# A fused recurrent-attention kernel: another order for the start of its first stage, hinted loop branches, moved transfers and key products

## What is computed

```python
xn = _layernorm(x, axis=-1)
s = _L0_attn_ref(xn, ...)          # recurrent attention, then a gated MLP
g = _silu(_L0_ffn_ref(xn, ...))    # 8 low-rank experts, softmax gate
x = x + s * g
# in _L0_ffn_ref
h = jax.nn.relu(jnp.einsum('bsd,de->bse', x, W1) + b1)
alpha = jax.nn.softmax(jnp.einsum('bse,ek->bsk', h, W2) + b2, axis=-1)
vx = jnp.einsum('krd,bsd->bskr', V, x)
uvx = jnp.einsum('kdr,bskr->bskd', U, vx)
out = jnp.einsum('bsk,bskd->bsd', alpha, uvx)
# in _L0_attn_ref: q, k, gk (decay), v, g from rmsnorm(x); then per token
S = S * jnp.exp(gt)[..., None] + kt[..., None] * vt[..., None, :]
ot = jnp.einsum('bhk,bhkd->bhd', qt, S)
```

## Time and profile before

| what | value |
|---|---|
| runs | 1780.17, 1783.14, 1783.19 us; median 1783.14 |
| profiled execution | 1781.37 us, its span 1779.6 us |
| TensorE busy | 1652.1 us, 93% of the span |
| VectorE, ScalarE, GpSimd busy | 48%, 32%, 10% |
| mean granted clock of TensorE | 0.980 |

### The profile page before, as it was taken

The page is one execution under the profiler, slowest core; times in us unless marked ns, Lnnn a source line. Parts: engine busy times, 40 slices in busy tenths (PEclk is TensorE's granted clock), DMA queues, the critical chain, the costliest instruction groups (busy, mean ns, idle before and its releaser), DMA issues. The chain is left out here.

```text
span 1779.6 us, 30533 instructions
## 1 busy us (share of the span) xinstructions
PE 1652.1 (93%) x12304; PEld 1291.5 (73%) x12304; DVE 847.2 (48%) x1348; ACT 562.3 (32%) x959; POOL 172.4 (10%) x201
## 2 busy tenths in 40 slices
PE   4999999869999999999996499999999999999998
PEld 3777777647767767677675387878787878787886
DVE  3655455336776857758564455232242414141413
ACT  3333333225544625435242343122212121212110
POOL 5780000021010010110000000000000000000000
PEclk9999999989999999999997799999999999999999
DMA  7243333020022020120110322303030303020110
GB/s 152 81 124 95 82 85 93 24 83 32 2 79 79 1 79 27 53 79 1 74 37 13 124 89 101 118 0 118 0 118 0 118 0 118 0 92 26 34 61 24
DMA packets 49100, 111.87 MB, mean 63 GB/s; under 512 B 12704, under 2 KB 24048, under 8 KB 40816
## 3 DMA queue, kind: packets, MB, share of 16 engines
q1 hardware_dynamic: 45104, 89.44, 15.7%
q10 hardware_dynamic: 2304, 16.78, 2.3%
q0 software_dynamic: 1600, 4.25, 1.2%
HBM read 76.89 MB, written 33.57 MB: 62 GB/s over the span
## 5 line engine op out<-in xcount | busy, mean ns | idle before, releaser
L1255 DVE TENSOR_TENSOR m_h<-m_ps,m_silu 128x512 f32<-128x512 f32 x88 | 60.8, 691 | 426.5 <-PE m_ps L1405 426.5
L1403 PE MATMUL m_ps<-m_xshi,m_w1hi 128*128 128x512 f32 x352 | 143.4, 407 | 7.3 <-DVE m_xslo L1248 6.0
L1331 ACT ACTIVATE m_silu<-m_ps 128x512 f32<-128x512 f32 x88 | 52.5, 597 | 289.6 <-PE m_ps L1405 288.8
L1403 PE MATMUL m_ps<-m_xshi,m_w3hi 128*128 128x512 f32 x352 | 140.4, 399 | 2.3 <-ACT m_silu L1331 2.3
L1404 PE MATMUL m_ps<-m_xslo,m_w1hi 128*128 128x512 f32 x352 | 139.8, 397 | 0.0
L1405 PE MATMUL m_ps<-m_xshi,m_w1lo 128*128 128x512 f32 x352 | 139.6, 396 | 0.0
L1404 PE MATMUL m_ps<-m_xslo,m_w3hi 128*128 128x512 f32 x352 | 139.5, 396 | 0.0
L1405 PE MATMUL m_ps<-m_xshi,m_w3lo 128*128 128x512 f32 x352 | 139.5, 396 | 0.0
L855 POOL TENSOR_TENSOR row<-row,a_r 128x512 f32<-128x512 f32 x32 | 41.6, 1335 | 618.0 <-DMA a_r<-scratch_r 618.0
L1376 POOL TENSOR_TENSOR m_sq_sum<-m_sq 128x512 f32<-128x512 f32 x8 | 10.4, 1298 | 782.8 <-ACT m_sq L1314 782.8
L1403 PEld LDWEIGHTS m_ps<-m_xshi,m_w1hi 128*128 128x128 f32 x352 | 66.5, 189 | 26.6 <-issue 9.2
(11 more groups left out here) (247 smaller groups left out, 3844.9 us busy)
## 6 DMA issues: line engine op xcount, KB each, us to landing
row<-scratch_xn SPq DMA_DIRECT2D x16, 1024.0 KB, 5.2
row<-scratch_xmid SPq DMA_DIRECT2D x16, 1024.0 KB, 7.2
m_xt<-in_L_attn_W SPq DMA_DIRECT2D x33, 256.0 KB, 3.2
f_xt<-in_L_attn_x SPq DMA_DIRECT2D x8, 1024.0 KB, 10.2
scratch_xn<-row SPq DMA_DIRECT2D x8, 1024.0 KB, 8.9
scratch_gate<-row ACTq DMA_DIRECT2D x8, 1024.0 KB, 3.9
scratch_xmid<-row ACTq DMA_DIRECT2D x8, 1024.0 KB, 3.9
row<-scratch_gate SPq DMA_DIRECT2D x8, 1024.0 KB, 9.7
```

Source lines behind the costliest of these rows:

```text
L1255: dve.tensor_tensor(h[n], dense.region(f"b{j}"), silu[n], ALU.mult).then_inc(dense.taken_sem(f"b{j}"), 1)
L1331: act.activation(silu[n], dense.region(f"a{j}"), ACT.Silu).then_inc(dense.taken_sem(f"a{j}"), 1)
L1403: pe.matmul(ps, wh, xh, start=k == 0, stop=False)
```

## The change

1. The constants move into the first stage's own GpSimd program. ScalarE and TensorE wait only for the first three steps (identity, epsilon); the block and its meeting are gone.
2. Each row of x is loaded by four transfers of 128 tokens, and VectorE's statistics wait for each piece alone. V is loaded second, before b1; b2 last. ScalarE waits for b1 alone.
3. V is turned after the first hidden product and U after the third; ScalarE splits them before the second and the fourth result. TensorE's passes over non-existent results move ahead of the turning of x or behind U.
4. All loops of all engines are opened with a hint for the branch at their end (line 139 before).
5. In attention `k1` moves to chunk 0, `q0` to chunk 1, and `q1` stays alone in chunk 2.
6. The store of the attention's sum moves from ScalarE to SyncE: it is issued in the next row, once that row's mixing of its last chunk is done. The load of `xn` follows it. The next row's `xa` is now loaded ahead of both.

```diff
-    with eng.Fori(1 if peel else 0, n - 1) as i:
+    with eng.bass.Fori(1 if peel else 0, n - 1, engines=bass.OrderedEngineSet([eng.engine]), hint_back_edge=True) as i:
...
-    with ExitStack() as ctx:
-        s_fill = ctx.enter_context(nc.semaphore("s_fill"))
-        block = ctx.enter_context(nc.Block())
...
+    pass
+
+
+def fill_constants(pool, consts, D, s_fill):
+    ident, hmask, causal, avg32, avg_all, ones, eps = consts
...
+        nonlocal n
+        n += 1
+        ins.then_inc(s_fill, 1)
+        pool.wait_ge(s_fill, n)
...
+    select(ident, ALU.not_equal, 0, [[-1, P]], 1, 1.0)
+    step(pool.memset(eps, EPS))
+    assert n == FIRST_CONSTANTS
+
...
+    step(pool.memset(ones, 1.0))
...
-                          ("vxlo", KT), ("x_in", 16), ("xn_out", 16), ("r1_out", 16)):
+                          ("vxlo", KT), ("xn_out", 16), ("r1_out", 16),
+                          *((f"x_in{t}", 16) for t in range(TT))):
...
+            fill_constants(pool, consts, D, s_fill)
             background(ctx, pool)
...
             def load(i):
                 sp.wait_ge(*turn.ready_before(f"xn{LAST}", i))
-                sp.dma_start(xt, row(x, i).rearrange("o (tt p) d -> p (o tt) d", p=P)).then_inc(count.sem("x_in"), 16)
+                for t in range(TT):
+                    sp.dma_start(xt[:, t, :], row(x, i)[:, t * P:(t + 1) * P, :].rearrange("o p d -> p (o d)")).then_inc(count.sem(f"x_in{t}"), 16)
...
             def weights(_):
                 sp.dma_start(w1_in, W1.rearrange("(k p) n -> p k n", p=P)).then_inc(s_w1, 16)
+                sp.dma_start(v_in, V.rearrange("(m a) r d -> (a r) m d", a=P // R)).then_inc(s_v, 16)
                 sp.dma_start(b1_sb, b1.rearrange("(kt p) -> p kt", p=P),
-                             allow_slow_non_contiguous=True).then_inc(s_small, 16)
+                             allow_slow_non_contiguous=True).then_inc(s_b1, 16)
                 sp.wait_ge(s_zero, 1)
                 sp.dma_start(w2[:, :, 0:E], W2.rearrange("(kt p) e -> p kt e", p=P)).then_inc(s_small, 16)
-                sp.dma_start(b2_sb, b2.partition_broadcast(P)).then_inc(s_small, 16)
-                sp.dma_start(v_in, V.rearrange("(m a) r d -> (a r) m d", a=P // R)).then_inc(s_v, 16)
                 for m in range(KT):
                     sp.dma_start(u_in[:, m, :].rearrange("p (k r) -> p k r", r=R),
                                  U[:, m * P:(m + 1) * P, :].rearrange("k p r -> p k r")).then_inc(s_u, 16)
+                sp.dma_start(b2_sb, b2.partition_broadcast(P)).then_inc(s_small, 16)
...
-                dve.wait_ge(*count.at("x_in", i))
                 for t in range(TT):
+                    dve.wait_ge(*count.at(f"x_in{t}", i))
                     dve.bn_stats(stats[:, t, :], xt[:, t, :]).then_inc(count.sem("stats"), 1)
...
             def hidden(i):
-                for m in range(KT):
+                first = isinstance(i, int) and i == 0
+                for m in range(KT):
+                    if first and m in (1, KT - 1):
+                        for n in range(KT if m > 1 else 0, 2 * KT if m > 1 else KT):
+                            split_turned(n)
                     act.wait_ge(*dense.ready(f"h{m}", i))
                     act.activation(h1[:, m, :], dense.region(f"h{m}"), ACT.Relu,
                                                        bias=b1_sb[:, m:m + 1]).then_inc(dense.taken_sem(f"h{m}"), 1)
...
-                act.wait_ge(s_small, 48)
-
-            def vu_parts(_):
-                for n, (src, hi, lo) in enumerate(vu_pieces):
-                    act.wait_ge(s_turned, n + 1)
-                    act.activation(hi, src, ACT.Copy).then_inc(s_whi, 1)
+                act.wait_ge(s_b1, 16)
...
-            loop_parts(act, NB, {"norm": norm, "w1": w1_parts, "xn": fill_xn, "h": hidden, "vu": vu_parts},
-                       body)
+            act.wait_ge(s_fill, FIRST_CONSTANTS)
+            loop_parts(act, NB, {"norm": norm, "w1": w1_parts, "xn": fill_xn, "h": hidden}, body)
...
-            def turn_weights(_):
-                pe.wait_ge(*turn.taken(f"xn{LAST}", 0))
-                for w, (s_in, need, src) in enumerate(((s_v, 16, v_in), (s_u, 16 * KT, u_in))):
-                    pe.wait_ge(s_in, need)
...
-                pe.wait_ge(s_wlo, KT + len(vu_pieces))
+            def turn_weights(w):
+                s_in, need, src = ((s_v, 16, v_in), (s_u, 16 * KT, u_in))[w]
+                pe.wait_ge(s_in, need)
...
             def hidden(i):
+                first = isinstance(i, int) and i == 0
                 linear(i, "h", w1, xn_hl, (0,), "xnlo")
                 for m in range(1, KT):
+                    if first and m == 1:
+
+                        pe.wait_ge(*turn.taken(f"xn{LAST}", 0))
+                        turn_weights(0)
+                    if first and m == LAST:
+                        turn_weights(1)
+                        pass_over(pe, dense, us, -1)
+                        pass_over(pe, turn, ["turned"] + alphas, -1)
                     linear(i, "h", w1, xn_hl, (m,))
...
-            parts = {"xn": turn_row, "h": hidden, "vu": turn_weights}
+            parts = {"xn": turn_row, "h": hidden}
             def before(part):
+                if part == "xn":
+                    pass_over(pe, dense, ["logit"] + vs, -1)
+                    pe.wait_ge(s_fill, FIRST_CONSTANTS)
                 if part == "h":
                     pe.wait_ge(s_wlo, KT)
-                    pass_over(pe, turn, ["turned"] + alphas, -1)
-                if part in ("h", "body"):
-                    pass_over(pe, dense, {"h": ["logit"] + vs, "body": us}[part], -1)
+                if part == "body":
+                    pe.wait_ge(s_wlo, KT + len(vu_pieces))
+                    pe.wait_ge(s_small, 32)
...
-        order = [(None, ["kt0"]), ("k0", ["k0"]), (None, ["ds0", "kt1"]), ("k1", ["k1"]),
-                 (None, ["ds1", "var0", "kt2"]), ("q0", ["q0"]), ("q1", ["q1"]), (None, ["ds2", "var1"]),
+        order = [(None, ["kt0"]), ("k0", ["k0"]), ("k1", ["k1"]), (None, ["ds0", "kt1"]), ("q0", ["q0"]),
+                 (None, ["ds1", "var0", "kt2"]), ("q1", ["q1"]), (None, ["ds2", "var1"]),
...
+            def store(i):
+                sp.wait_ge(*dense.taken(f"o{LAST}", i))
+                sp.dma_start(row(xmid_d, i).rearrange("o p m t -> p (o m) t"), xn).then_inc(count.sem("xmid_out"), 16)
+
             def body(i, ahead):
+
                 ahead("xa")
+                sp.wait_ge(*mix.ready(NC - 1, i))
+                if not isinstance(i, int):
+                    store(i - 1)
+                elif i > 0:
+                    store(i - 1)
                 sp.wait_ge(*count.at_before("xmid_out", i))
                 sp.dma_start(xn, row(xn_d, i).rearrange("o p m t -> p (o m) t")).then_inc(count.sem("xn_in"), 16)
+
             def next_phase(_):
                 sp.wait_ge(*count.at("xalo", NB - 1))
+                sp.wait_ge(*count.at("xmid_out", 0))
...
             sp.sem_inc(count.sem("xa_in"), 16)
             load_r1(0)
-            loop_parts(sp, NB, {"xa": load}, body, skip=next_phase, first=False)
+            loop_parts(sp, NB, {"xa": load}, body, peel=True, skip=next_phase, first=False)
+            store(NB - 1)
...
+                    if name == "q":
+                        act.wait_ge(*count.at_before("mqh", i))
                     act.wait_ge(*dense.ready(f"{name}{g}", i))
...
-                    for part in (("k0",), ("k1",), ("q0", "q1"), ())[c]:
+                    for part in (("k0", "k1"), ("q0",), ("q1",), ())[c]:
                         ahead(part)
...
                 ahead("g")
-                act.wait_ge(*dense.taken(f"o{LAST}", i))
-                act.dma_start(row(xmid_d, i).rearrange("o p m t -> p (o m) t"), xn).then_inc(count.sem("xmid_out"), 16)
...
-                        for part in (("k0",), ("k1",), ("q0", "q1"))[c]:
+                        for part in (("k0", "k1"), ("q0",), ("q1",))[c]:
                             ahead(part)
                         weights(i, c + 1)
```

More of the change, by code:

```diff
@@ L16 @@
 GATE_SCALE = 1.0 / 16.0
+FIRST_CONSTANTS = 3
 class Counts:
@@ new lines, in make_constants, with step, select @@
+    pass
+def fill_constants(pool, consts, D, s_fill):
+    ident, hmask, causal, avg32, avg_all, ones, eps = consts
+    n = 0
+    def step(ins):
+        nonlocal n
+        n += 1
+        ins.then_inc(s_fill, 1)
+        pool.wait_ge(s_fill, n)
+    def select(ap, op, base, pattern, cm, fill):
+        step(pool.affine_select(out=ap, in_=ap, compare_op=op, fill=fill, base=base,
+                                pattern=pattern, channel_multiplier=cm))
+    step(pool.memset(ident, 0.0))
+    select(ident, ALU.not_equal, 0, [[-1, P]], 1, 1.0)
+    step(pool.memset(eps, EPS))
+    assert n == FIRST_CONSTANTS
+    step(pool.memset(hmask, 1.0))
+    select(hmask, ALU.is_ge, 0, [[-16, 8]], 1, 0.0)
+    select(hmask, ALU.is_ge, 15, [[16, 8]], -1, 0.0)
+    step(pool.memset(causal, 1.0))
```

(36 more changed lines are left out.)

2 lines of the change are left out of this document (1 added, 1 removed).

## The result

The changed kernel takes 1775.27 us (median of seven runs, 1769.64 to 1777.0), the kernel before 1783.19 (seven runs, 1780.17 to 1790.38). The ratio is 0.9948 with a 95% interval of 0.9929 to 0.9967: about 9 us faster, where 21.6 were forecast. The time lies outside the forecast range, above it. The profiled execution took 1777.0 us, its span is 1775.3.

A forecast was written before the change was run, and what follows sets the result against it. TensorE was taken to set the pace, with losses at the start and in many short attention waits; 11.0 (start) + 9.7 (attention) = 20.7 off the profiled 1781.37 gave 1760.7, stated as a 1761.5 us median, range 1753 to 1770.

The forecast's parts named there:

- The start: Up to the first logits: first hidden product at 18.9 instead of 26.74, 7.8 saved, and 2.3 more to the first logits.
- the bandwidth sum: Loading at the start: x lands at 8.6, W1 and V take 4.1 each, so b1 lands at 16.8.
- the estimate from the Trainium skill's figures: Loading x in pieces: four take 8.0 instead of 6.15, everything behind lands 1.8 later, the start saves 9.2.
- The first row's clock: First row of the first stage: with only 0.9 idle before the first logits the clock stays up, 1.9 saved.
- 0.08 per us, 1.0 lost: Early first-stage rows: starting earlier, they overlap more of GpSimd's preparation, at 0.08 per us, 1.0 lost (bounds 0 and 3).
- k1 and q1: Attention: k1 in chunk 0 saves 6.1 of mask waits; q1 alone adds a 1.31 wait before chunk 3, 9.2 lost.
- 12.0 saved: Attention: the hint and the moved transfers end TensorE's waits for issue, 12.0 saved (bounds 4 and 12).
- the scaling starts some 5 us earlier and is over when the states come: Attention: with xa loaded ahead of xn, GpSimd's scaling no longer meets the states, avoiding a 3.2 wait in each row.
- rival C: Attention: store and load of xn form one chain behind the mixing and make the kernel slower, about 1801 us; chance 0.03.
- the signs that the prediction named: First hidden product, first and next logits, attention mask waits, TensorE's branch, issue waits, rows about 71 us, scaling, third stage.
- Rival A: Attention: the branch's 3 us stay and about half of the 12.0 with them, 1767.5 us; chance 0.13.
- rival B: Attention: VectorE's chain bounds, GpSimd's scaling meets the states, 3.2 wait before chunk 3 in each row, 1774 us; chance 0.10.

The follow-up runs named there:

- the work left out: The changed kernel without GpSimd's centring of Wv and scaling by ln1 (38 us of work): 1764.51 us, ratio 0.9890.
- held to other places: The changed kernel with early first xn load, k1 and q0 in old chunks, and GpSimd's preparation waiting three times for VectorE's splits: 1753.95 us, ratio 0.9837.
- the old places: The changed kernel with k1 back in chunk 1 and q0 back in chunk 2: 1766.62 us, ratio 0.9894.
- early load alone: The changed kernel, but row 0's load of xn does not wait for that row's last mixing: 1764.26 us, ratio 0.9883.
- both repairs: The changed kernel with row 0's xn load not waiting for the mixing, and k1 and q0 in their old chunks: 1762.67 us, ratio 0.9881.
- whole x: The changed kernel with x in four pieces for row 0 only and one transfer for other rows: 1774.7 us, ratio 0.9947.

## Why the prediction was wrong

- **The start, right.** First hidden product at 18.10 (18.9 forecast), first logits at 36.61 (37.4 by the sum's terms). The changed kernel issues b1 at 5.85 and it takes 10.2: it landed at 16.07, where the bandwidth sum had 16.8. The pieces of x let VectorE begin at 5.71, 2.7 after the first issue where the whole transfer had 5.6; the last piece landed 5.6 after the first issue. W1 landed 3.8 us behind x (4.1 before), so the estimate from the Trainium skill's figures ("DMA: Bandwidth & Descriptors", Measured), 1.8 us later, did not come true here.
- **The first row's clock, half right.** 0.8 of 1.9 was saved. The clock stayed at 1.00 (0.96 before), but TensorE waited three times for VectorE's splits, 1.1 us in all, with GpSimd at work beside them.
- **"0.08 per us, 1.0 lost", wrong.** The term was a mean over 51 us of GpSimd's work beside the rows, and the price depends on what the work meets. Starting 11 us earlier, together with GpSimd's wait of 7.25 us for Wo, put the splits of the third row beside the last two pieces of Wo, and the loss was 4.6, above the bound of 3. Held against two undisturbed rows (78.5 us), the two rows lost 4.1 in the kernel before, 8.7 in the changed one, 0.3 with the work left out and 1.4 with it held to other places.
- **k1 and q1, right in kind.** The forecast had a net loss of 3.1 (6.1 against 9.2); the old places show 4.1 in the six rows, and 3.8 in the first (74.61 with the early load alone, 70.81 with the old places too; a wait of 1.78 without a partner, in the middle of the state products of chunk 1, is gone there). The new wait was sized rightly (1.40 for 1.31), the removed one was not: with the other edits it is 0.7, not 1.04. So a wait's worth changes with the other edits.
- **"12.0 saved" by hint and transfers, right in kind, too small.** The hint saves 3.26 a row once the new transfers are in, 19.5 in six rows, and 1.5 a row alone. The forecast looked at the branch, and missed that the fetches of a whole body end. That the six rows gained 15.9 where 11.0 were forecast is the net of this term, too small, and of the products' term, too good.
- **The step that failed: the first attention row.** The prediction said of the moved transfers "the scaling starts some 5 us earlier and is over when the states come", and costed them by the later rows. There it came true: VectorE's state updates take at most 0.49 us in the changed kernel, up to 1.50 before. It took the first row for one whose "loads already stood as they will". The order of SyncE's program says otherwise: in row 0 the load stands behind a mixing that it doesn't need. The row was forecast to lose 1.3 us and lost 12.3, and these 11.0 are most of the 16.3 by which the traced execution misses the sum of 20.7. The early load alone takes 7.9 of the 12.3 us back. So does the hint on TensorE alone (8.3): the loss needs the late load and the hint on another engine at once, ScalarE's by the place of the wait, and that hint was costed at nothing. The other 4 are the products' new places (above). None of the rivals had it; rival C named the same chain but looked for it in the store. Nor had the signs that the prediction named: start, masks, branch, steady rows and third stage came out as named or nearly so (a first row of 40.4 us for 39 to 40, attention rows of 70.0 for 71), and none of them singles out the first attention row. Rival A (the hint does nothing) and rival B (3.2 before chunk 3) are refuted by the rows above.
- **What stays open.** From the last logits to the first small product it is 93.57 and 94.25 us in two executions of the changed kernel, 90.59 before. TensorE is idle 23.1 us there in both executions (23.2 before), so no wait is new. It is busy 3.1 us longer, at a granted clock of 0.89 where the kernel before had 0.92:

```profile
321.29:414.86 93.57, 70.43 (x284) 52.47 (x283) 38.80 (x60) 33.68 (x56) 10.86 (x8) 0.89 0.11 40
```

```profile
328.38:418.97 90.59, 67.36 (x283) 49.95 (x283) 38.79 (x60) 33.33 (x56) 10.89 (x8) 0.92 0.13 53
```

The first line is of the changed kernel, the second of the one before. Kernels with the same program in this place fell on either side (91.06 with both repairs, 94.11 with the first alone), and no edit sorts them. The 1.9 us of the last attention row weren't tried on their own. There, too, TensorE's idle time is that of before (30.4 and 30.5 us), and the granted clock is 0.73, where it was 0.79. Of the 1.4 in the third stage only this is shown: 785.6 to 786.6 in six executions of five kernels with moved transfers and all hints, 784.4 and 784.5 with the hint on TensorE alone, but also 784.1 and 785.0 in two with all hints (whole x, light preparation), 784.5 in the kernel before with all hints, and 784.5 in the changed kernel without any.

## What to carry to other kernels

When a wait or a transfer is moved in a loop, walk through the turn that is written out apart (first or last) as well: there the reason for the wait may not exist, and the wait does. Price the work of an engine beside another's by the instruction on the path that it will meet, not by its mean, and if that engine has slack, hold it until that instruction is past. Hint the branch on the engine whose body is fetched again in each turn, and look at the others' first turn before they get one.

## What had not been expected of the hardware

- With a hint at the back edge, the whole run has 25 instruction packets of 16 KB in place of 79, and issue waits of 1 to 2 us in the middle of the body went, not only those behind the branch.
- With the hint on all engines ScalarE has a wait without a partner in the first turn of the attention loop: 1.2 to 1.6 us, and 4.1 to 4.6 where two megabytes of loads are under way. Without a hint on it there is none.
- A VectorE running sum over 128x128 takes 0.34 us alone (1.37 for four) and 1.37 beside GpSimd; a subtraction over 128x512 0.69 and 1.64. The Trainium skill, "SBUF — State Buffer", SBUF: two separate sides, has the two engines lock a port pair that they share; both rows agree with that.
